# Infini-attention block with a mixture of experts on one core: the attention result's halves are transposed by a transposing DMA, the output projection runs one round later, and the stores are by tiles and fewer

## The reference

```
h = layernorm(x) * (1 + ca) + sa
x = x + ga * infini_attention(h)         # 16 heads of 16, segments of 64 tokens
h = layernorm(x) * (1 + cb) + sb
x = x + gb * moe(h)                      # 8 experts, the best 2 of each token

infini_attention, by segment:
    A_mem = sigma(q) @ M / (sigma(q) . z + eps)
    A_dot = softmax(q k' / 4, causal) @ v
    A     = beta * A_mem + (1 - beta) * A_dot
    M, z  = updated with sigma(k), v - V_prev
    out   = A @ W_o.T
```

## Time and profile before

| | |
|---|---|
| median of 3 runs | 1305.98 us |
| the profiled execution | 1306.74 us, its span 1304.9 us |
| PE busy | 1160.5 us, 89% of the span |
| POOL busy | 941.2 us, 72% |
| DVE busy | 906.2 us, 69% |
| ACT busy | 706.5 us, 54% |
| granted PE clock, mean | 0.939 |

### The profile page before, as it was taken

One profiled execution on the slowest core, in us unless ns is written; L12 is line 12 of the kernel. 1 busy time (PEld: TensorE's weight loads), 2 busy tenths in 40 slices (PEclk: granted clock), 3 DMA queues, 4 the chain that ended last, 5 costly groups with the idle time before them and its releaser, 6 DMA issues. The chain is left out here.

```text
span 1304.9 us, 53730 instructions
## 1 busy us (share of the span) xinstructions
PE 1160.5 (89%) x19576; PEld 983.5 (75%) x19576; DVE 906.2 (69%) x2481; ACT 706.5 (54%) x1393; POOL 941.2 (72%) x989
## 2 busy tenths in 40 slices
PE   4689999999899899999723799999999999999995
PEld 1477777888777777777513588888888888888884
DVE  2589999999998999989888545444444544444542
ACT  2377888888888888878634133233333323333331
POOL 3168999999998989989841466666676666767653
PEclk8599999999999999989755899999999999999998
DMA  8323343334333433433445676777878787777770
GB/s 217 84 68 80 105 127 113 95 105 118 103 109 97 115 102 101 116 96 109 112 96 169 127 136 129 145 130 125 130 142 136 130 144 123 138 138 139 136 110 1
DMA packets 203977, 153.09 MB, mean 117 GB/s; under 512 B 103930, under 2 KB 181842, under 8 KB 203602
## 3 DMA queue, kind: packets, MB, share of 16 engines
q1 hardware_dynamic: 163042, 81.90, 25.4%
q0 software_dynamic: 32592, 56.75, 25.2%
q10 hardware_dynamic: 8096, 11.01, 3.1%
HBM read 63.58 MB, written 44.04 MB: 82 GB/s over the span
## 5 line engine op out<-in xcount | busy, mean ns | idle before, releaser
L1289 PE MATMUL psum<-xT,xall 128*128 128x256 f16 x3408 | 385.3, 273 | 13.5 <-DMA xT<-grow 13.3
L1289 PEld LDWEIGHTS psum<-xT,xall 128*128 x3408 | 334.1, 98 | 53.6 <-issue 14.1
L1349 POOL DMA_INDIRECT out<-late,sidx x142 | 230.7, 1625 | 160.1 <-DVE late L1340 99.4
L1297 ACT ACTIVATE sg<-psum 128x512 f32<-128x512 f32 x142 | 84.6, 596 | 282.7 <-PE psum L1289 204.2
L1302 DVE SCALAR_TENSOR_TENSOR late<-psum,sg 128x512 f32<-128x512 f32 x142 | 98.2, 691 | 171.3 <-ACT sg L1297 118.1
L1269 POOL DMA_INDIRECT grow<-moe_rows,gidx x142 | 150.5, 1060 | 86.1 <-DVE sidx L1155 43.1
L1323 PE MATMUL psum<-w2s,hT 128*128 x1704 | 199.3, 274 | 3.8 <-DVE w2s L1375 3.5
L1323 PEld LDWEIGHTS psum<-w2s,hT 128*128 128x128 f16 x1704 | 167.4, 98 | 24.3 <-issue 4.3
L1313 DVE TENSOR_TENSOR hT<-late,hT 128x512 f16<-128x512 f32 x142 | 98.8, 696 | 98.8 <-ACT hT L1309 84.2
L1309 ACT ACTIVATE hT<-late 128x512 f16<-128x512 f32 x142 | 89.4, 629 | 113.7 <-DVE late L1302 98.5
L673 POOL TENSOR_TENSOR pT<-sc,pT 128x1024 f16<-128x1024 f32 x64 | 136.6, 2134 | 10.5 <-ACT pT L669 10.3
(11 more groups left out here) (255 smaller groups left out, 2300.9 us busy)
## 6 DMA issues: line engine op xcount, KB each, us to landing
stk<-qk SPq DMA_DIRECT2D x384, 64.0 KB, 2.8
moe_rows<-hrows SPq DMA_DIRECT2D x128, 128.0 KB, 3.0
out<-xall SPq DMA_DIRECT2D x128, 64.0 KB, 2.5
raw<-in_w ACTq DMA_DIRECT2D x26, 256.0 KB, 3.1
xall<-in_x ACTq DMA_DIRECT2D x16, 256.0 KB, 4.0
raw<-in_w SPq DMA_DIRECT2D x8, 512.0 KB, 9.5
xall<-in_x SPq DMA_DIRECT2D x8, 384.0 KB, 8.2
grow<-moe_rows,gidx POOLq DMA_INDIRECT x142
```

The source lines that it names most:

```text
L1289: i = k.e.matmul(bank[:, n * LONG:(n + 1) * LONG], w13s[:, bass.ds(ex_reg * (G * 4 * I) + ((2 * c + b_) * 2 * I + col), P)], xT[:, k.x, a, ...
L1297: done(k.e.activation(sg[:, half, :], bGate[half][:, :], ACT.Silu, scale=1.0 / W_SCALE), "sg")
L1349: k.e.indirect_dma_start(out_rows, bass.IndirectOffsetOnAxis(ap=sidx[:, n:n + 1], axis=0), yo[:, k.v, q, :], None, bounds_check=B * T - 1, ...
```

## The change

What it does:

- `a_trans` and `a_act` are gone. A new stage of SP, `a_turn` (lag 9, last in SP's list), waits for `alo` of its tile and `Wo` of the tile two before, and issues one transposing DMA from `ah` to `aT`. `w_o` waits for this DMA (`k.turned()`).
- `w_o` has lag 7 where it had 6, and all that follows the output projection moves one round later on every engine.
- `moe_rows` is now ordered by tile: one DMA of 128 rows writes a tile, where two of 64 rows did. The tile of `xall` goes to `out` every second segment, two segments at once (`OUT_SEGS = 2`); `store` has lag 14.
- The expert weights (eight floats a row) go out in one DMA where there were eight, twice in the program.
- The token numbers are rows of `moe_rows`; DVE turns them into rows of `out` in some ten small operations before the first scatter.
- The wait for `s_out` moves from the load of `raw` to ACT's conversion of it.

The core of the diff:

```diff
 def store(k):
     k.wait_apart(("hlo",))
+    k.e.dma_start(rows_dram[k.t * P:(k.t + 1) * P, 0:2 * D], hrows[:, k.j, :].bitcast(F32)).then_inc(s_st[k.j], 16)
+    if k.s % OUT_SEGS < OUT_SEGS - 1:
+        return
+    done_before = k.s // OUT_SEGS
+    if done_before:
+        k.e.wait_ge(s_out[k.j], done_before * 32)
+    some = slice(k.s - OUT_SEGS + 1, k.s + 1)
     for b2, toks in enumerate(HALVES):
-        k.e.dma_start(rows_dram[(2 * k.j + b2) * T + k.s * SEG:(2 * k.j + b2) * T + (k.s + 1) * SEG, 0:2 * D],
-                      hrows[toks, k.j, :].bitcast(F32)).then_inc(s_st[k.j], 16)
-    if k.s > 0:
-        k.e.wait_ge(s_out[k.j], k.s * 32)
-    for b2, toks in enumerate(HALVES):
-        k.e.dma_start(out[2 * k.j + b2, k.s * SEG:(k.s + 1) * SEG, :],
-                      xall[toks, k.t, :]).then_inc(s_out[k.j], 16)
+        k.e.dma_start(out[2 * k.j + b2, :, :].rearrange("(s t) d -> t s d", t=SEG)[:, some, :],
+                      xall[toks, :, :].rearrange("p (s j) d -> p s j d", j=NJ)[:, some, k.j, :]).then_inc(s_out[k.j], 16)
...
+def turned(self, back=0):
+    if self.t >= back:
+        self.e.wait_ge(s_aT[self.b], 16 * ((self.t - back) // 2 + 1))
...
-def a_trans(k):
-    k.wait("ahi")
-    k.wait("alo")
-    k.wait_banks("AT")
-    for n in range(2 * G):
-        i = k.e.transpose(bkAh[:, n * P:(n + 1) * P],
-                          ah[:, k.b, :, :].rearrange("p a d -> p (a d)")[:, n * P:(n + 1) * P], idh[:, :])
-    done(i, "AT")
-def a_act(k):
-    k.wait("AT")
-    k.wait("Wo", 2)
-    done(k.e.activation(aT[:, k.b, :, :, :].rearrange("p a c t -> p (a c t)"), bkAh[:, 0:2 * D], ACT.Copy), "aT")
+def a_turn(k):
+    k.wait_apart(("alo",))
+    k.wait_apart(("Wo", 2))
+    k.e.dma_start_transpose(aT[:, k.b, :, :, :].rearrange("p a c t -> p (a c) t"),
+                            ah[:, k.b, :, :].rearrange("p a d -> p (a d)")).then_inc(s_aT[k.b], 16)
 def w_o(k):
-    k.wait("aT")
+    k.turned()
     k.wait_banks("Wo")
...
-    "sync": [(4, stack_low), (3, stack_high), (13, store)],
-    "tensor": [(2, mem_mm), (11, h2_trans), (3, max_trans), (2, proj_v), (1, proj_qk), (4, pv), (6, a_trans),
-              (3, scores_by_key), (6, w_o), (0, t1), (2, scores), (3, update), (12, router)],
+    "sync": [(4, stack_low), (3, stack_high), (14, store), (9, a_turn)],
+    "tensor": [(2, mem_mm), (12, h2_trans), (3, max_trans), (2, proj_v), (1, proj_qk), (4, pv),
+              (3, scores_by_key), (7, w_o), (0, t1), (2, scores), (3, update), (13, router)],
...
-def weights_out(e, rows_dram, w8, s0, s1, s_w8):
-    for j in range(NJ):
-        for b2 in range(2):
-            dst = rows_dram[(2 * j + b2) * T + s0 * SEG:(2 * j + b2) * T + s1 * SEG, 2 * D:ROW].rearrange(
-                "(s t) e -> t s e", t=SEG)
-            src = w8[b2 * SEG:(b2 + 1) * SEG, :, :].rearrange("p (s j) e -> p j s e", j=NJ)[:, j]
-            e.dma_start(dst, src).then_inc(s_w8, 16)
+def weights_out(e, rows_dram, w8, t0, t1, s_w8):
+    e.dma_start(rows_dram.rearrange("(t p) e -> p t e", p=P)[:, t0:t1, 2 * D:ROW], w8[:, :, :]).then_inc(s_w8, 16)
...
-        e.tensor_scalar(gidx[:, :], rowf[:, :], 0.0, None, ALU.max)
-        link(e.tensor_scalar(hasf[:, :], rowf[:, :], 0.0, float(OOB + ID0), ALU.is_lt, ALU.mult))
-        e.tensor_tensor(sidx[:, :], rowf[:, :], hasf[:, :], ALU.add).then_inc(s_idx, 1)
+        e.tensor_scalar(gidx[:, :], rowf[:, :], 0.0, None, ALU.max).then_inc(s_idx, 1)
```

More of the change, by code:

```diff
@@ L53 @@
 NXT = 3
+OUT_SEGS = 2
 ROUND_X = 10
@@ L407, in attention @@
     names = ("stats aggr eps pow nmr xn lna T1 h1T h1L pqk pv qkh exq rel vhi vlo qlo sig scr mx mTr mTh mTl "
-             "sT exp phi plo memm den rec mV mA vpr skt upm umul madd PV pdn rcp ado aadd ahi alo AT aT Wo "
+             "sT exp phi plo memm den rec mV mA vpr skt upm umul madd PV pdn rcp ado aadd ahi alo Wo "
              "gat res st2 ag2 ep2 pw2 nm2 xn2 l2a l2b hhi hlo h2Tr h2T rtr lg").split()
@@ L414, in attention @@
     s_st = [sem(f"s_st{j}") for j in range(4)]
+    s_aT = [sem(f"s_aT{b_}") for b_ in range(2)]
     PER_SEGMENT = ("eps", "pow", "nmr")
@@ L428, in attention @@
              (("ado", 1),)),
-        "AT": ((("h1T", -5), ("h1L", -5),),
-             (("aT", 1),)),
         "sT": ((("mA", -1), ("mV", -1), ("skt", -1),),
@@ L434, in attention @@
              (("gat", 1), ("lg", 7),)),
-        "T1": ((("aT", 6),),
-             (("h1T", 1), ("h1L", 1),)),
+        "T1": ((("h1T", 1), ("h1L", 1),),
+             ()),
         "scr": ((("ado", 2),),
@@ L465, in arrived_before @@
                 self.e.wait_ge(sems[j], s * (16 * n) + 16 * n)
+        def turned(self, back=0):
+            if self.t >= back:
+                self.e.wait_ge(s_aT[self.b], 16 * ((self.t - back) // 2 + 1))
         def stored(self):
             if self.s > 0:
-                self.e.wait_ge(s_st[self.j], self.s * 32)
+                self.e.wait_ge(s_st[self.j], self.s * 16)
         def of_tile(self, rows):
@@ L784, in a_high @@
         k.wait("aadd")
-        k.wait("AT", 2)
+        k.turned(2)
         k.wait("alo", 2)
@@ L880, in attention @@
     program = {
-        "sync": [(4, stack_low), (3, stack_high), (13, store)],
-        "tensor": [(2, mem_mm), (11, h2_trans), (3, max_trans), (2, proj_v), (1, proj_qk), (4, pv), (6, a_trans),
-                  (3, scores_by_key), (6, w_o), (0, t1), (2, scores), (3, update), (12, router)],
+        "sync": [(4, stack_low), (3, stack_high), (14, store), (9, a_turn)],
+        "tensor": [(2, mem_mm), (12, h2_trans), (3, max_trans), (2, proj_v), (1, proj_qk), (4, pv),
+                  (3, scores_by_key), (7, w_o), (0, t1), (2, scores), (3, update), (13, router)],
         "vector": [(2, aggr), (9, mem_a), (9, mem_v), (0, stats), (9, v_rest), (9, v_new), (11, pv_den),
[L885 to L892, removed]
+                  (11, pv_scale), (11, pv_dve), (15, ln2_shift), (8, q_rest), (8, sigma), (14, resid),
+                  (9, row_max), (10, update_dve), (14, stats2), (7, h1t_rest), (8, mem_den), (9, max_rest),
+                  (14, aggr2), (8, mem_rec), (14, var_eps2)],
+        "scalar": [(6, qk_high), (6, qk_relu), (10, a_high), (0, var_eps), (6, qk_exp),
+                  (8, softmax_exp), (8, p_high), (5, h1t), (13, ln2_act), (18, logit_copy), (6, sk_act),
+                  (7, max_high), (14, rows_hi), (3, ln_act), (16, h2_act), (6, v_high)],
+        "gpsimd": [(12, p_rest), (8, ln_mult), (17, ln2_mult), (18, rows_lo), (16, ln2_scale), (12, update_add),
+                  (13, a_rest), (17, ln2_add), (3, ln_scale), (12, a_add), (15, res_add), (3, ln_shift)],
     }
@@ L902, in raw_load @@
         if half == 0:
-            for j in range(4):
-                e.wait_ge(s_out[j], 32 * (n + 1))
             if n >= NRAW:
@@ L912, in raw_high @@
             e.wait_ge(s_raw[n % NRAW], 32 * (n // NRAW + 1))
+            for j in range(4):
+                e.wait_ge(s_out[j], 32 * (n // OUT_SEGS + 1))
             w13_high(e, w13s, raw[:, n % NRAW, :], n).then_inc(s_rhi, 1)
@@ L1016, in _ @@
             e.wait_ge(e_placed, 2)
-            weights_out(e, rows_dram, early.w8, 0, EARLY // NJ, e_w8)
+            weights_out(e, rows_dram, early.w8, 0, EARLY, e_w8)
             for j in range(4):
-                e.wait_ge(s_st[j], 32 * NS)
+                e.wait_ge(s_st[j], 16 * NS)
             for j in range(4):
-                e.wait_ge(s_out[j], 32 * NS)
-            e.wait_ge(e_w8, 16 * B)
+                e.wait_ge(s_out[j], 32 * NS // OUT_SEGS)
+            e.wait_ge(e_w8, 16)
         @block.tensor
@@ L1059, in experts @@
     tend, ex_of = sb("tend", [P, E]), sb("ex_of", [P, NSLOTS])
+    rowf, hasf, seg_of, rest = [sb(n_, [P, NW]) for n_ in ("rowf", "hasf", "seg_of", "rest")]
     routing = ExitStack()
@@ L1081, in experts @@
     found16 = scratch("found16", [P, NW], F16)
-    rowf, hasf = scratch("rowf", [P, NW]), scratch("hasf", [P, NW])
     s_v, s_gap, s_exp = sem("r_v"), sem("r_gap"), sem("r_exp")
@@ L1101, in route_sync @@
         e.wait_ge(s_weights, 1)
-        weights_out(e, rows_dram, w8, EARLY // NJ, NS, s_w8)
+        weights_out(e, rows_dram, w8, EARLY, NT, s_w8)
     def route_vector(e):
@@ L1162, in route_vector, with whole @@
         link(e.tensor_tensor(oh_tile[:, :, :], bc(ex_of[:, :], E), bc_mid(iota[:, 3, 0:E], NSLOTS), ALU.is_equal))
+        def whole(found, step):
+            link(e.tensor_scalar(found[:, :], found[:, :], -(step - 1) / 2, 1.0 / step, ALU.add, ALU.mult))
+            link(e.tensor_scalar(found[:, :], found[:, :], ROUND, -ROUND, ALU.add, ALU.add))
+        link(e.tensor_scalar(hasf[:, :], rowf[:, :], 0.0, float(2 * OOB), ALU.is_lt, ALU.mult))
+        link(e.tensor_copy(seg_of[:, :], rowf[:, :]))
+        whole(seg_of, NJ * P)
+        link(e.scalar_tensor_tensor(out=rest[:, :], in0=seg_of[:, :], scalar=-float(NJ * P), in1=rowf[:, :], op0=ALU.mult,
+                                    op1=ALU.add))
+        whole(rest, SEG)
```

(13 more changed lines are left out.)

## The result

| | before | changed |
|---|---|---|
| median | 1305.48 us (4 runs) | 1721.78 us (4 runs, 1715.16 to 1727.70) |
| ratio | | 1.317, 95% interval 1.312 to 1.322 |
| the profiled execution, span | 1304.9 us | 1713.2 us |
| PE, DVE, ACT, POOL busy us | 1160, 906, 706, 941 | 1298, 916, 682, 934 |
| granted PE clock, mean | 0.939 | 0.802 |

What follows compares the result with a forecast made beforehand. PE, DVE and POOL, each 94% busy, were taken to bound the attention stage. A round of 8.30 + 6.38 + 2.0 = 16.68 us against 9.18 gave +435 over 58 rounds; 1306.7 + 435 + 18 - 0.4 = 1759, so 1758 us, range 1595 to 1875.

Steps and rivals of the forecast that it cites:

- The place of the wait: SP issues tile T's transposing DMA only after `scores_by_key` of T+4, directly behind which PE needs it; 58 rounds stall.
- The size of the stall: PE's wait ahead of `w_o`, from SP's issues to the DMA's landing: mean 6.38 us a round, ends 5.2 and 8.2.
- the landing: Time of the transposing DMA to its landing, a term of the stall: 3.38 us, bounds 2.2 and 4.8.
- The sign "5 to 8 us in each of 58 rounds": Expected in the profile after: PE idle this long before L802 (`w_o`), released by the DMA from `ah` to `aT`.
- The clock: PE runs slower after each stall, from `w_o` to `proj_qk`: 2.0 us lost a round, ends 0 and 2.67.
- my upper end of 2.67: Most the slower clock could cost a round: `w_o` to `proj_qk` in 7.33 us against 4.66.
- 8.30: PE's time in us from one projection to the next place of a projection, without the four transposes: 8.62 - 0.32.
- PE never regaining its clock: Rival: PE stays at the lower clock, a round takes 19.4 us, 1918 us in all; chance 8%.
- The last six tiles: Tiles with no `stack_high` ahead: 3 us more each for the DMA before the projection, +18 us; ends 0 and +22.
- The thinning of the stores: On SP, some three issues of 0.6 us a round fewer and one transposing issue more; taken as no effect.
- the upper end of the stall: Largest wait of PE ahead of `w_o` by the bounds of the terms: 8.2 us a round.
- The rival of a hidden landing: SP issues the DMA early enough, nothing waits, PE loses 0.32 us a round: 1295 us; chance 3%.

Runs made afterwards that it cites:

- the stores alone: The kernel before with only the change's other half (stores, weights, row numbers), halves still transposed on PE, no lag moved: 1301.10 us, ratio 0.996.
- e1_turn_first: The changed kernel with `a_turn` (lag 9) moved ahead of `stack_high` in SP's list, nothing else: 1340.87 us, ratio to before 1.025.
- e2_lag8: The changed kernel with `a_turn` left last in SP's list but at lag 8 instead of 9: 1315.84 us, ratio 1.008.

## Why the prediction was right

- **The place of the wait.** Right, tile by tile: in the 58 rounds L795 never comes ahead of the end of L657, PE waits 58 times, and moving one entry of SP's list, in place, by a round or both, with nothing of the work changed, gives back 381 to 420 us.
- **The size of the stall.** 6.38 us a round against 5.35 measured (5.18 from the end of L657 to `w_o`, and the 0.17 by which the projection used to overlap its predecessor). The term that was off most is the landing: 3.38 taken, 2.5 measured. The sign "5 to 8 us in each of 58 rounds" holds only where stores to `out` stand ahead (6.0); the other rounds wait 4.6 us, and the first ones 4.0. By the rule of the Trainium skill (Advanced Engine Details and Errata, section X-Bar Transpose (TRN2)) it should be that of regular DMAs; the 2.5 between 2.2 (stores) and 2.7 (`stk` copies) agrees, and the single row of before was taken beside gathers. At full pace the same DMA has medians of 3.6 to 4.0 on SP's queue (the stores to `moe_rows` there 3.6 to 3.7) but 2.7 on ACT's, so pace alone doesn't set it; what does stays open.
- **The clock.** 2.0 taken. The round shown has 7.48 against 4.66 us, and over the rounds of tiles 0 to 56 the mean is 7.36, so 2.7 measured, at my upper end of 2.67. The two errors nearly cancel, which was luck: 8.30 + 5.35 + 2.70 = 16.35 us a round against 16.68, and from tile 0's projection to tile 57's a round is 16.35 on average.
- **PE never regaining its clock** did not happen: from `proj_qk` on the round shown is at full speed (1.50 us for L559, as in the earlier trace rows).
- **The ends.** The last six tiles cost nothing (forecast +18, measured -6). That is my lower end, another engine holding these rounds; POOL is busy 35.5 of 40 us from 1040, which fits, but no run tests it. Tile 0's projection comes 8.0 us later: 4.55 are its own stall, one of my 58, and the other 3.5, with its place one round later, I had not counted.
- **Two slips in the working**, of no weight for the forecast. The thinning of the stores takes two issues a round from SP, not three (256 stores before, 128 now). And the upper end of the stall, 8.2 us, doesn't follow from its terms: with a landing of 4.8 it is 7.8, and with the store at 1.18 as well 8.4.
- **The rival of a hidden landing**, faster by 20 us at most: with the issue early enough it came out as 1302 us, no gain beyond that of the stores alone. The rule of the Trainium skill (DMA: Bandwidth & Descriptors, section Rules for kernel authors), to issue early and wait late, holds here: the round later at which `w_o` waits was not enough while the issue stood behind the event that it should precede, and 5.2 us a round were paid.

How much of the 2.5% of `e1_turn_first` is the buffer `ah` and how much the longer chain stays open: a kernel with more buffers for `ah` was not run. Nor was one that leaves SP's list alone and gives `w_o` a lag of 8: its projection would stand behind the scores one tile later than the event that releases the DMA, the same distance as in `e2_lag8`.

## What to carry to other kernels

Before a transfer is moved to a queue that executes in order, write down what each entry ahead of it waits for, with the tile's number, and compare it with what the consumer's engine does just before it needs the data; if they are the same event, the whole way from it to the landing is paid in every round, until one of the two is moved by a round. A long wait in PE's stream (here 4 to 6 us) is paid twice, in idle time and in the slower clock behind it. A DMA that takes over a copy also holds its source buffer for the whole landing time, so buffers that were deep enough for an engine may not be for it.

## What the runs showed of the hardware

A transposing DMA of 128 rows of 512 16-bit numbers, between two places of SBUF, occupied SP for 1.2 us, twice as long as the plain copies (0.6). It landed 2.5 us after its issue in all kernels in which PE stalled for it in every round. At nearly full pace its median was 3.6 to 4.0 us on SP's queue and 2.7 on ACT's. One store of 128 rows of 2 KB took 0.52 us of SP, less than each of the two of 64 rows it replaced (0.60). It landed 2.2 us after its issue in the stalled kernel, but 3.5 to 3.7 at full pace, where the smaller ones had 3.0; so the larger store cost less of SP and did not land sooner. Behind waits of 1.98 us and 2.33 us PE's matmuls ran at the clock of 0.50, but behind one of 2.49 us at 1.00, each between stretches of nearly unbroken work.
